# Moving one tile's stacking transfers behind the first tile's maxima rows, in a gated cross-attention and mixture-of-experts kernel

## The reference, cut to what matters

```
x = x + tanh(g_xattn) * attention(layernorm(x), ctx)     # 32 batches, T=128 rows, D=128, 16 heads of 8
        q = (xn @ Wq + bq), k = (xfn @ Wk + bk), v = (xfn @ Wv + bv);  ctx has N=77 rows of 96
        softmax(q k / sqrt(8)) v, head by head
x = x + tanh(g_ffn) * ffn(layernorm(x))                  # 8 experts, the best 2 of each row
        logits = x @ w_router; top 2; softmax of the two
        sum over the two of prob * (relu(x @ w1[e]) ** 2 @ w2[e])
```

## Time and profile before

| what | value |
|---|---|
| median of three runs | 309.58 us (308.25 to 310.35) |
| profiled execution | 310.32 us |
| its span in the trace | 308.5 us |
| mean granted TensorE clock, as a share of full | 0.978 |
| busy: TensorE matmuls, VectorE, ScalarE, GpSimd | 92%, 73%, 59%, 40% of the span |

### The profile page before, as it was taken

The page is one execution under the profiler, slowest core; times in us unless marked ns, Lnnn a source line. Parts: engine busy times, 40 slices in busy tenths (PEclk is TensorE's granted clock), DMA queues, the critical chain, the costliest instruction groups (busy, mean ns, idle before and its releaser), DMA issues.

```text
span 308.5 us, 7846 instructions
## 1 busy us (share of the span) xinstructions
PE 284.8 (92%) x2827; PEld 237.7 (77%) x2827; DVE 224.5 (73%) x898; ACT 181.7 (59%) x415; POOL 123.3 (40%) x243
## 2 busy tenths in 40 slices
PE   7887498988999999999999999999999999999994
PEld 5555386767878888888888887888888888788784
DVE  7786149678678986888688868886767766756675
ACT  2586244656765656566656576566756546565573
POOL 8445326377136721671277227522442211221110
PEclk9999559999999999999999999999999999999999
DMA  3336912294729335772757372807391540070011
GB/s 65 97 82 104 111 31 64 72 102 68 257 79 131 77 132 184 106 114 74 241 80 110 106 240 59 114 8 228 116 128 15 153 162 2 7 290 19 3 34 35
DMA packets 19471, 31.62 MB, mean 102 GB/s; under 512 B 5321, under 2 KB 11722, under 8 KB 19432
## 3 DMA queue, kind: packets, MB, share of 16 engines
q1 hardware_dynamic: 12080, 22.08, 30.8%
q0 software_dynamic: 3392, 6.75, 10.9%
q10 hardware_dynamic: 3960, 2.29, 3.9%
HBM read 18.94 MB, written 2.21 MB: 69 GB/s over the span
## 4 chain that ended last, share of the span: by engine, by line
PE 53%; DVE 19%; DMA 11%; issue 6%; ACT 4%; POOL 3%; ACTq 2%; SPq 1%; DVEq 0%; POOLq 0%
PE y L614 12%; PE c L566 8%; PE ab L522 6%; DMA ks<-k_hi 5%; PE s L543 4%; DVE u L1237 4%; DMA qs<-mT 3%; DVE negm L1120 3%; PE ab L589 2%; DMA gb<-gates_scratch 2%; PE ab L581 2%; PE h L607 2%; PE h L609 2%; PE h L608 2%; DVE xn L1165 2%
## 5 line engine op out<-in xcount | busy, mean ns | idle before, releaser
L1120 DVE TENSOR_REDUCE negm<-ab 128x4 f32<-128x308 f32 x128 | 60.1, 474 | 40.4 <-PE ab L522 39.2
L875 ACT ACTIVATE p<-s 77x512 f32<-77x512 f32 x128 | 74.2, 583 | 22.9 <-PE s L543 22.7
L543 PEld LDWEIGHTS s<-qs,ks 104*77 104x77 f32 x512 | 54.9, 152 | 17.4 <-DMA qs<-mT 4.5
L543 PE MATMUL s<-qs,ks 104*77 104x128 f32 x512 | 59.8, 241 | 6.7 <-DMA qs<-mT 4.2
L614 PE MATMUL y<-w2s,hs 128*128 128x128 f32 x448 | 60.6, 279 | 1.4 <-ACT hs L880 1.4
L614 PEld LDWEIGHTS y<-w2s,hs 128*128 128x128 f32 x448 | 55.4, 193 | 3.5 <-ACT hs L880 2.6
L1477 POOL TENSOR_SCALAR rs<-mv 128x1 f32<-128x1 f32 x32 | 7.3, 227 | 122.5 <-DVE mv L1159 122.5
L522 PE MATMUL ab<-ks,qs 96*128 96x312 f32 x128 | 49.0, 388 | 3.7 <-DMA ks<-k_hi 1.8
L880 ACT ACTIVATE hs<-u 128x512 f32<-128x512 f32 x56 | 35.0, 625 | 11.4 <-DVE u L1237 10.6
L1237 DVE SCALAR_TENSOR_TENSOR u<-h,gb 128x512 f32<-128x512 f32 x56 | 38.0, 678 | 2.4 <-PE h L609 1.5
L566 PE MATMUL c<-p,vs 77*32 77x128 f32 x1024 | 35.4, 280 | 0.0
(11 more groups left out here) (146 smaller groups left out, 501.5 us busy)
## 6 DMA issues: line engine op xcount, KB each, us to landing
gb<-gates_scratch SPq DMA_DIRECT2D x14, 768.0 KB, 5.5
gb<-gates_scratch SPq DMA_DIRECT2D x14, 256.0 KB, 3.4
qs<-q_hi SPq DMA_DIRECT2D x11, 256.0 KB, 7.5
out_dram<-y_out POOLq DMA_DIRECT2D x7, 256.0 KB, 5.9
x_sb<-in_x_dram POOLq DMA_DIRECT2D x6, 256.0 KB, 3.6
qs<-q_lo SPq DMA_DIRECT2D x6, 256.0 KB, 9.4
ks<-k_hi SPq DMA_DIRECT2D x34, 39.0 KB
ks<-k_lo POOLq DMA_DIRECT2D x32, 39.0 KB, 3.3
```

What stands on the lines that cost most here:

```text
L543: mm = nc.tensor.matmul(p[0:N, T * i:T * i + T], ks[:, par, c, i, NP * j:NP * j + N], qs[:, par, c, T * j:T * j + T], start=True, stop=True)
L875: nc.scalar.activation(p32[:, m % LR, :], src, ACT.Exp).then_inc(p_done, 1)
L1120: nc.vector.tensor_reduce(negm[:, :, c], bank_ab[bank][:, 0:J * NP].rearrange("t (i n) -> t i n", n=NP)[:, :, 0:N], AX.X, ALU.max, negate= ...
```

## The change

Three groups of work move, all of them for the second tile or later, and one group of identity matmuls goes.

- SyncE: `stack_k(1, 1)`, five transfers, goes from step (-1, 2), where it stands between the maxima rows of batches 0 and 1 of the first tile, to step (0, 0), behind the maxima rows of batch 2.
- ScalarE: `stack_q_rows(1, 1)`, two transfers, and `clear_some` of the second half of the second tile's `vs` go from step (-1, 3), ahead of the first exponential, to step (0, 0), behind the fourth exponential of the first batch and ahead of the first exponential of the second batch.
- GpSimd, step (0, 0): before, `mark_values`, `stack_first_low_q`, `load(2, 0)`, `low_expert(0)`, `low_expert(1)`; after, `stack_first_low_q`, the two `low_expert`, `mark_values`, `load(2, 0)`.
- TensorE: the `keep_on` of two matmuls (four instructions) in the middle of step (0, 1) goes.

```diff
@@ sync @@
-                    if (i, j) == (-1, 2):
+                    if (i, j) == (0, 0):
                         stack_k(1, 1)
-                    if (i, j) == (0, 0):
                         unit_rows(1)
@@ tensor @@
-                    if (i == 0 and j > 0) or (i == 1 and j < 2):
+                    if (i == 0 and j > 1) or (i == 1 and j < 2):
                         keep_on(bank_h[0 if (i, j) == (0, 3) else 1], 2)
@@ scalar @@
                     if (i, j) == (-1, 3):
                         max_store(*near[2])
                         evacuate_q(1, 1)
-                        stack_q_rows(1, 1)
-                        clear_some(1, slice(G // 2, G))
                         exponent(*near[1], 0)
                         continue
...
                     if near[0]:
                         exponent(*near[0], 3)
+                    if (i, j) == (0, 0):
+                        stack_q_rows(1, 1)
+                        clear_some(1, slice(G // 2, G))
@@ gpsimd @@
                     if (i, j) == (0, 0):
+                        stack_first_low_q()
+                        low_expert(0)
+                        low_expert(1)
                         mark_values(pool, nc.gpsimd, 1)
-                        stack_first_low_q()
                         load(2, 0)
                     if (i, j) == (0, 1):
                         load(3, 1)
-                    if (i, j) in ((0, 0), (0, 1), (0, 2), (1, 0)):
-                        part = ((0, 0), (0, 1), (0, 2), (1, 0)).index((i, j))
+                    if (i, j) in ((0, 1), (0, 2), (1, 0)):
+                        part = 1 + ((0, 1), (0, 2), (1, 0)).index((i, j))
                         low_expert(2 * part)
                         low_expert(2 * part + 1)
```

## The result

The changed kernel takes 311.39 us (median of 14 runs, 310.08 to 314.04) beside 310.30 us (14 runs, 307.68 to 311.49). The ratio, from runs made beside each other, is 1.0063, with a 95% interval of 1.0036 to 1.0091: slower by 0.6%, inside the 1% band that I had called no change, and on the other side of it from the forecast 308.4. The forecast started from the 309.58 of three runs; from 310.30 it would have been 309.1. Ratios compare runs made beside each other and leave out executions over 1.5% above the fastest of their kernel, which the medians and the lists keep, so a ratio can differ from the quotient of two medians. The profiled execution took 314.04 us, the slowest of the 14, with a span of 312.2 us.

A forecast was written before the change was run, and what follows sets the result against it. TensorE was taken to bound the kernel, with one dip around 30 to 45 us. The second tile's first score matmul 3.7 us earlier, less 2.5 us of low clock, gains 1.2 us: 309.6 to 308.4 us, range 304.9 to 311.6.

The forecast's parts named there:

- three signs of "right": Longest early TensorE wait ends on second-tile transfers at 40 to 44 us; batch 1 maxima land within 4; clock low from about 40.
- What bounds the kernel: TensorE, busy nearly throughout, with one dip around 30 to 45 us: 4.24 us idle, then 9.7 us of work at low clock.
- Passed on one to one: From 53 us on TensorE paces each slot, so whatever the first 50 us gain or lose reaches the end in full.
- The first tile's rows and exponentials: TensorE can run the transposed scores of batch 1 from 30.6 us instead of 35.83, a gain of 5.2 us.
- When TensorE arrives: TensorE reaches the second tile's first score matmul at 37.5 us, including about 1 us of new idle time for ScalarE.
- The landing: The second tile's last transfer, the second `q_hi`, lands at 41.8 us (40.2 to 43.7), so TensorE idles 4.3 us.
- The clock again: The low clock returns for work from 41.8 us on and costs 2.5 us in slot (0, 2), range 2.2 to 3.3.
- VectorE's wait for ctx: Third tile's ctx lands at 41 to 43 us and VectorE stands there; costs nothing up to 43.4, one to one after.
- SyncE's row transfer, GpSimd's order, identity matmuls: Batch 3's later row transfer, `low_expert` ahead of `mark_values`, and the removed identity matmuls: each put at nothing.
- The clock holds: Rival: the clock stays full or comes back soon; gain 3.7 us, 305.9, down to 304.3 us; chance 0.20.
- Starved: Rival: the load slows the query transfers, the second tile's matmul stays at 45.5 us; 312.6 to 313.1 us; chance 0.12.
- The change doesn't do what it says: Rival: batch 1's rows stay slow through GpSimd's seven key transfers; between that and no effect 309.6 us; chance 0.08.

The follow-up runs named there:

- whole wait filled: Changed kernel with identity matmuls added: one and one in step (0, 0), fifteen in the new wait; 309.84 us, 1.0012.
- keys alone: Kernel before with only SyncE's part of the change: five key transfers behind the maxima rows of batch 2; 307.11 us, 0.9900.
- filled early load: Changed kernel with the third tile's load first in step (0, 0) and six identity matmuls more, four in the new wait; 306.49 us, 0.9833.
- keys alone with the early load: Kernel before with SyncE's part of the change alone, and the third tile's load issued first by GpSimd in step (0, 0); 306.83 us, 0.9892.
- the load first: Changed kernel with GpSimd issuing the third tile's load first in step (0, 0), at 28.43 and 29.20 us; 307.60 us, 0.9893.
- the filled old wait: Kernel before with nine identity matmuls in its old 4.24 us wait, ahead of the transposed scores of batch 1; 309.67 us, 0.9998.
- the filled versions: Kernels with identity matmuls put into TensorE's waits, such as the changed kernel with eleven in the new wait, 311.80 us.
- the load behind the keys: Changed kernel with GpSimd issuing the third tile's load only once SyncE's five key transfers have landed; 313.31 us, 1.0138.
- the matmuls put back: Changed kernel with the four removed identity matmuls of step (0, 1) put back; 310.36 us, 1.0032.
- The fill in the keys-alone version with the early load: "keys alone with the early load" plus three identity matmuls ahead of the transposed scores in step (0, 0); 309.55 us, 0.9964.
- the four kernels with the whole change: Changed kernel with the load first in step (0, 0): unfilled 307.60 us, with two single fills 307.74, with four more 306.49, with eight more 306.51.
- the spare transfer: Changed kernel with the third tile's load in step (-1, 0) and an unread 256 KB load at 28.4 us; 310.15 us, 0.9996.
- the queries' half alone: Kernel before with the change's queries, clear, GpSimd order and identity matmul parts, the keys staying in step (-1, 2); 308.07 us, 0.9922.
- the kernel with eleven: Changed kernel with thirteen identity matmuls more: one and one in step (0, 0), eleven in the new wait; 311.80 us, 1.0009.
- the early load with eight: Changed kernel with the load first in step (0, 0), two single identity matmuls there and eight in the new wait; 306.51 us, 0.9868.

## Why the prediction was wrong, step by step

The mechanism came as forecast: the old wait went, a new one of the second tile's transfers came, and the clock was low behind it. All three signs of "right" were there: the longest wait ends on the keys at 42.2, the first tile's rows landed before they were needed, and the clock is low from 39.9, though for 13.65 us and not about 10. What failed is a size in the sum, and it turned its sign.

- **What bounds the kernel.** The dip was read rightly. "Passed on one to one" from 53 us on was not. In the traces, the lead over the kernel before at its 53.76 and again at its 84.47, us: whole wait filled 3.4 and 2.3; keys alone 3.7 and 1.2; filled early load 3.7 and 0.0; keys alone with the early load 3.8 and 3.9; kernel after -0.7 and -3.6. What is left at 84 is within 0.6 us of the final difference in all of these. So the slots between 64 and 88 us take something back in most traces, 2.2 to 3.7 us in the four in which the clock falls there again. My sum had no term for it.
- **The first tile's rows and exponentials.** Forecast 30.6, measured 30.69.
- **When TensorE arrives.** Forecast 37.5, measured 35.5. I had let the turn of heads wait 1 us for ScalarE behind the two issues and the clear. ScalarE issued the queries at 30.07, 1 us earlier than I had it, beside its last exponentials, and that wait didn't come. The other 1 us is the work itself: from the transposed scores of batch 1 to the new wait it took 4.8 us at full clock, where I had scaled it to 5.9 by 7.04 to 9.24, the ratio that fails below. Neither cost anything, the landing decides, but the hole is 6.7 us and not 4.3.
- **The landing.** Forecast 41.8 from bounds 40.2 to 43.7, measured 42.2. The size is right and the transfer is not, so the size is in part luck: I had the second `q_hi` last, with 10.0 us. The queries took 4.2 and 8.2 us and landed at 38.95; the five key transfers of 39 KB, issued last, were late. Of the 3.7 us forecast, 3.3 came. That all these bytes share the same engines is what the Trainium skill says ("DMA: Bandwidth & Descriptors", "Issuing engines are not separate DMA queues"); the trace agrees, since three places for the keys or the load moved the wait between the first tile's rows, the keys and ctx. It doesn't follow that order is worth nothing: the load first was worth 3.5 us at the landing.
- **The clock again: the term that failed.** I priced it at 2.5 us, range 2.2 to 3.3; it cost 4.0, 0.80 ahead of `values` of batch 1 and 3.17 in slot (0, 2). Both factors were too small. The low stretch over work was 11.3 us, not 9.7: I had taken 9.7 from "unbroken work until it is back", and after the 6.7 us hole it took longer. And one us of it cost 0.35 us (4.0 in 11.3), where I had 2.2 for a slot of 9.24, that is 0.24. I had that price from two different slots: (0, 1) at the low clock against the mean of later ones at full. Slot (0, 1) is shorter than those, 5.40 us at full clock, as the filled old wait shows, so its price was 3.84. Gain 3.3 less 4.0 is the sign of the result: a sum of two terms of like size and opposite sign, the second without a row at both clocks. With 0.35 for the 9.7 us forecast it would have been 3.4 against a gain of 3.7, an estimate of nearly no change.
- **How long it is low.** Over all executions, twice the missing share of the mean clock times the span gives a median of 19.8 us after and of 13.6 to 14.8 in the groups of before; I had assumed the same stretch elsewhere. Where the further low time of the unprofiled executions lies isn't known. In the filled versions the time goes with it: from mean clock 0.999 to 0.982, 10.5 us more at the low level, it is 307.6 to some 312, 0.4 us each; in the filled early load, 1.0 to 0.989, 6.7 us, it is 302.9 to 306 and 307, 0.5 to 0.6 each. In the kernel after it doesn't: the three executions at 0.977 took 311.4 to 311.9 us, the five at 0.965 to 0.967 310.1 to 311.4. So the mean clock alone doesn't tell the time; what work lies under it counts. The Trainium skill ("TensorE: Matmul & The Clock Gate", "Terms") puts the loss at the share of the clock taken away, half of the throttled time: 6.8 us for the 13.65 of the kernel after. The trace has 4.0, since 2.4 us of it lay over the wait and matmuls aren't all that a slot consists of.
- **VectorE's wait for ctx** was forecast as standing there without being on the path; it was 5.38 us, until 40.70, and with the clock full slot (0, 2) took its 7.35 us in spite of it. The kernel with the load behind the keys shows the case in which it decides.
- **SyncE's row transfer, GpSimd's order, identity matmuls** at nothing: no wait of the profile speaks against the first two, and the matmuls put back changed nothing beyond the interval.
- **The rivals.** "The clock holds" at 305.9 didn't come by itself. Made by hand, with the wait filled whole, it gave 308.46 in the profiled execution, with a full clock. That is 1.9 us below the 310.32 of the kernel before, where I had worked out 3.7: the landing brought 3.4, and 1.5 were given back later. The median, 309.84, is higher still. "Starved" didn't come: the matmul ran at 42.24, not 45.5. The kernel with the load behind the keys is as slow as its price, 313.3, but by another way, the late ctx. "The change doesn't do what it says" didn't come either: TensorE found the rows of batch 1 there at 30.69.
- **What I didn't weigh at all** is that two halves of a change can each be good and undo each other. Both shorten the same chain up to one landing. The keys alone take the old wait away and spend the low clock on work that had time; with the queries moved as well TensorE comes to the landing early, at full clock, with nothing to do. The fill in the keys-alone version with the early load made that exchange on purpose and cost 2.7 us.

Open: why the load issued at 28.4 gives a landing at 38.7 to 39.4 in the four kernels with the whole change, and 40.98 in the filled one with the keys alone, and no load nearby one of 40.9 to 41.3. Engines kept busy beforehand aren't it (the spare transfer landed them at 42.0). Open too is which execution gets a late second fall of the clock, and why, and so how much of the 0.6% comes from behind 54 us: the two terms above make 0.7 us.

What beats both kernels: keys alone (307.1, 0.990) and with the early load (306.8, 0.989), the queries' half alone (308.1, 0.992), the early load on the whole change (307.6, 0.989), and that with its waits filled (306.5 twice, 0.983 and 0.987). Their intervals overlap, so they aren't told apart.

## What to carry to other kernels

Where a chain ends at a transfer's landing, ask with which clock TensorE meets it: bringing TensorE there earlier buys nothing and can cost the clock behind the landing, while slow work in front of it can be free. Price the low clock from one and the same slot at both levels, not from two slots. Try the halves of such a change alone before the whole. If a wait can't be avoided, a fill has to reach its end and no further: 1.9 us left open cost the clock, and a fill that ran over cost its overrun. Even then it is no promise: with the wait filled whole, four executions of twelve had a mean clock of 1.0. And follow a lead past the place where it was won: here up to 3.7 us of it went between 64 and 88 us.

## What the runs showed of the hardware that was not expected

- The clock fell without a long break before it. Before the fall at 42.4 in the kernel with eleven, TensorE had stood for 1.94 us only, after 5 us of unbroken identity matmuls. Before the fall at 43.0 in the early load with eight, its longest waits since 33.5 were two of 0.39 us, and it was busy for 6.8 of the 7.5 us from 35.5.
- One us at the low level cost 0.46 us in slot (0, 1) (9.24 against 5.40 us, 8.3 of them low) and 0.33 us in slot (0, 2) (10.52 against 7.35, 9.6 of them low).
- It came back late: 13.65 us low in both profiled kernels, and between 3.4 and 23.9 us in others. With the queries alone TensorE was busy for 18.6 of the 20 us from 32 to 52, and the clock stayed low until the last window of 2 us.
- Executions of one kernel differ by whether the clock falls, and their times by more than most of the variants: six executions of one program took 302.86 us (mean clock 1.0) to 310.45 us (0.977).
- Transfers of 39 KB from on-chip memory to on-chip memory took 2.3 us when little else was under way (GpSimd's three, issued from 26.9 to 28.5 us in the kernel after), and five of them 11.3 us from the first issue to the last landing beside 256 KB ones.
